# Cached attention as one unrolled line on turned layouts, and grouped attention's values as three products of 256 columns

## The reference, cut to what matters

```python
def _L0_xattn_ref(x, mask, k_cache, v_cache, wq, wk, wv, wo):
    q, k_new, v_new = (jnp.einsum('bsd,ed->bse', x, w) for w in (wq, wk, wv))
    k = jnp.concatenate([k_cache, k_new], axis=1)
    v = jnp.concatenate([v_cache, v_new], axis=1)
    scores = jnp.einsum('bqd,bkd->bqk', q, k) / math.sqrt(256)
    out = jnp.einsum('bqk,bkd->bqd', jax.nn.softmax(scores, axis=-1), v)
    return jnp.einsum('bqd,ed->bqe', out, wo)
...
x = x + _L0_xattn_ref(_layernorm(x), mask, ctx_2048, ctx_2048, wq, wk, wv, wo)      # cached attention
x = x + _L0_ffn_ref(_layernorm(x), ...)       # 32 experts, top 4
x = x + _L1_xattn_ref(_layernorm(x), ctx_2048, ...)   # 16 heads of 128, 4 groups of keys: grouped attention
x = x + _L1_ffn_ref(_layernorm(x), ...)       # weights of -1, 0, 1; 8-bit activations
return x
```

## Time and profile before

| what | us |
|---|---|
| runs shown: median (lowest) | 1720.77 (1715.43) |
| the profiled execution, its own time | 1719.92 |
| its span, first to last instruction | 1718.2 |
| cached attention, until the experts' first transfer | 219.7 |
| grouped attention, about | 1116 |

### The profile page before, as it was taken

The page is one execution under the profiler, slowest core; times in us unless marked ns, Lnnn a source line. Parts: engine busy times, 40 slices in busy tenths (PEclk is TensorE's granted clock), DMA queues, the critical chain, the costliest instruction groups (busy, mean ns, idle before and its releaser), DMA issues. The chain is left out here.

```text
span 1718.2 us, 26126 instructions
## 1 busy us (share of the span) xinstructions
PE 1471.8 (86%) x9363; PEld 1327.4 (77%) x9366; DVE 1185.7 (69%) x2437; ACT 992.3 (58%) x2070; POOL 549.4 (32%) x458
## 2 busy tenths in 40 slices
PE   5788735888867898999999989999999999999945
PEld 4777734887756887888988889888888988888823
DVE  3444556888856877777777767777767777777657
ACT  2434414778744655576666666665656656666626
POOL 1011123344434532243232234332323423222125
PEclk8888966999987999999999999999999999999978
DMA  4111035899931312020010101100201001000010
GB/s 161 39 39 39 1 124 171 294 295 300 317 115 40 65 32 64 7 53 21 28 40 20 52 20 40 41 20 25 67 7 53 20 28 38 12 18 22 23 52 25
DMA packets 79334, 121.40 MB, mean 71 GB/s; under 512 B 16740, under 2 KB 59912, under 8 KB 78696
## 3 DMA queue, kind: packets, MB, share of 16 engines
q1 hardware_dynamic: 74648, 107.28, 19.6%
q0 software_dynamic: 4560, 12.46, 3.1%
HBM read 107.72 MB, written 11.99 MB: 70 GB/s over the span
## 5 line engine op out<-in xcount | busy, mean ns | idle before, releaser
L1688 ACT ACTIVATE ga_pT<-ga_ps_t 128x512 fp32r<-128x512 f32 (+1 forms) x512 | 243.8, 516 | 242.8 <-PE ga_ps_t L1928 242.1
L1823 DVE TENSOR_TENSOR ga_pT<-ga_ps_t,ga_pT 128x512 fp32r<-128x512 f32 (+1 forms) x512 | 279.9, 582 | 89.8 <-ACT ga_pT L1688 87.5
L1696 ACT ACTIVATE ga_probs<-ga_ps_s,ga_neg_max 128x1200 f32<-128x1200 f32 (+1 forms) x256 | 235.7, 927 | 107.3 <-DVE ga_neg_max L1844 107.0
L1928 PE MATMUL ga_ps_t<-all_eye,ga_probs 128*128 128x128 f32 (+1 forms) x1664 | 227.0, 274 | 3.0 <-DVE ga_pT L1823 3.0
L1928 PEld LDWEIGHTS ga_ps_t<-all_eye,ga_probs 128*128 128x128 f32 (+1 forms) x1664 | 195.2, 141 | 17.7 <-DVE ga_pT L1823 4.7
L1839 DVE TENSOR_REDUCE ga_part_max<-ga_ps_s 128x1 f32<-128x1200 f32 x128 | 178.5, 1394 | 7.8 <-PE ga_ps_s L1879 7.2
L1879 PE MATMUL ga_ps_t<-side_w_kv,side_encT 128*128 128x256 f32 (+1 forms) x1170 | 163.9, 289 | 13.4 <-DVE ga_pT L1823 8.6
L1964 PE MATMUL ga_ps_m<-ga_pT,side_v 128*128 128x512 f32 (+1 forms) x416 | 160.8, 417 | 13.5 <-DVE ga_out_n L1857 13.2
L1879 PEld LDWEIGHTS ga_ps_t<-side_w_kv,side_encT 128*128 128x128 f32 (+1 forms) x1170 | 146.5, 188 | 26.0 <-DVE ga_pT L1823 13.1
L1879 PE MATMUL ga_ps_s<-side_kT,ga_qT 128*128 128x400 f32 (+1 forms) x768 | 159.2, 357 | 5.2 <-ACT ga_probs L1696 5.1
L1964 PE MATMUL ga_ps_m<-ga_pT,ga_v 128*128 128x512 f32 (+1 forms) x416 | 157.9, 411 | 6.0 <-DVE ga_out_n L1857 4.5
(11 more groups left out here) (304 smaller groups left out, 3004.6 us busy)
## 6 DMA issues: line engine op xcount, KB each, us to landing
ex_raw<-in_L_ffn_packed SPq DMA_DIRECT2D x63, 704.0 KB, 6.2
side_w_q_raw<-in_L_xattn_Wq SPq DMA_DIRECT2D x16, 512.0 KB, 4.6
side_w_q_raw<-in_L_xattn_Wo SPq DMA_DIRECT2D x16, 512.0 KB, 4.7
ga_inv_rows<-ga_inv_row SPq DMA_DIRECT2D x64, 128.0 KB, 3.1
mix_y_rows<-ex_y SPq DMA_DIRECT2D x63, 128.0 KB, 4.5
ca_cache<-in_ctx SPq DMA_DIRECT2D x4, 1536.0 KB
side_enc<-in_ctx_turned SPq DMA_DIRECT2D x12, 512.0 KB, 5.1
ca_f_raw<-in_L_ffn_turned SPq DMA_DIRECT2D x3, 1024.0 KB, 11.0
```

Of the source, the lines that this page charges most:

```text
L1688: nc.scalar.activation(dst(HI), src, ACT.Copy, scale=scale).then_inc(read, 1)
L1696: nc.scalar.activation(dst, src, ACT.Exp, bias=neg_max[:, n % 2:n % 2 + 1], accum_out=half_sum[:, n % 4, k:k + 1]).then_inc(exped, 1)
L1823: nc.vector.tensor_tensor(dst(LO), src, f32(dst(HI)), ALU.subtract).then_inc(empty, 1)
L1928: mm = nc.tensor.transpose(out[0:top, i * P:(i + 1) * P], probs[step % PB][:, tile * P:tile * P + top], eye[:, :])
```

## The change

`cached_attention` is written anew in the manner of the grouped attention: 8 steps n (b = n // 2, t = n % 2) and 3 draining ones, a plan that all engines walk, three banks of `ps_t`, three buffers of probabilities. TensorE's program is this plan:

```diff
+    def turned_probs(n):
+        if n % 2 == 0:
+            u, order = n // 2 - 1, [(0, 0), (1, 0), (0, 1), (1, 1)]
+        else:
+            u, order = (n - 3) // 2, [(0, 2), (0, 3), (1, 2), (1, 3)]
+        return [("pT", (t, k), u) for t, k in order] if 0 <= u < B else []
+    def weighed_at(n):
+        u, half = ((n - 3) // 2, 0) if n % 2 else (n // 2 - 2, 1)
+        return [("weigh", (half, piece), u) for piece in range(2)] if 0 <= u < B else []
+    def step_plan(n):
+        b, t = n // QT, n % QT
+        turns, values = turned_probs(n), weighed_at(n)
+        first = [("scores", 0, n)] if n < N else []
+        if t:
+            to = b + 1
+            xT, q, k = ([(kind, 0, to)] if to < B else [] for kind in ("xT", "q", "k"))
+            return first + turns[0:2] + xT + values[0:1] + q + turns[2:3] + k + values[1:2] + turns[3:4]
...
+        return first + turns[0:2] + values[0:1] + turns[2:3] + values[1:2] + turns[3:4] + v + y + f
+    plan = {-1: [("xT", 0, 0), ("q", 0, 0), ("k", 0, 0)]}
```

```diff
+            sp.dma_start(x_sb[:, 0:QT, :], tokens[:, 0:QT, :]).then_inc(x_in, 16)
+            load_weight(Q)
+            load_keys(0)
+            load_weight(K)
+            sp.dma_start(x_sb[:, QT:B * QT, :], tokens[:, QT:B * QT, :]).then_inc(x_rest_in, 16)
+            load_weight(V)
+            load_weight(O)
+            sp.wait_ge(cleared, 1)
+            load_cache(0, 0)
+            load_cache(0, 1)
+            load_ternary(0)
+            load_keys(1)
+            for b in range(1, B):
+                load_cache(b, 0)
+                if b + 1 < B:
+                    load_keys(b + 1)
+                load_cache(b, 1)
+                store_ternary(b - 1)
+                if b < W:
+                    load_ternary(b)
```

```diff
+                        ring(("xT", 0, to))
+                        keys_high(to, 0)
+                        keys_high(to, 1)
+                        ring(("q", 0, to))
+                    for e in turns[2:3]:
+                        ring(e)
...
+                        keys_high(to, 2)
+                        ring(("k", 0, to))
+                    for e in turns[3:4]:
+                        ring(e)
...
+                        keys_high(to, 3)
...
+                        cache_high(b - 1, 1)
...
+                        ternary_sign(b - 1)
```

In the grouped attention:

```diff
-        ps_m = ps("ps_m", [P, 2, S])
+        ps_m = ps("ps_m", [P, S])
...
-                nc.scalar.activation(out_n[:, :], ps_m[:, 1, :], ACT.Copy).then_inc(b_here, 1)
+                nc.scalar.activation(out_n[:, :], ps_m[:, :], ACT.Copy).then_inc(u_here, 1)
...
-            def add_parts(u):
-                dve.wait_ge(b_here, u + 1)
-                nc.vector.tensor_tensor(out_n[:, :], ps_m[:, 0, :], out_n[:, :], ALU.add).then_inc(u_here, 1)
...
-                if n % 2 and 0 <= (n - 5) // 2 < UNITS:
-                    add_parts((n - 5) // 2)
...
-                    nc.tensor.matmul(ps_m[:, :, :], values[0:top, HI, tile, :], pT[0:top, :, tile, :],
-                                     start=tile == 0, stop=False)
-                    mm = nc.tensor.matmul(ps_m[:, 0, :], values[0:top, LO, tile, :], pT[0:top, HI, tile, :],
-                                          start=False, stop=tile == KT - 1)
+                    mm = product(ps_m[:, :], lambda s: values[0:top, s, tile, :], lambda s: pT[0:top, s, tile, :],
+                                 tile == 0, tile == KT - 1)
```

More of the change, by code:

```diff
@@ L82, in cached_attention @@
     ABS_FLOOR = 1e-5
-    assert DC == 2 and QT == 2 and FULL == 12 and NB == 4
+    W, FK = ffn_turned.shape[1], ffn_turned.shape[2]
+    Q, K, V, O = range(4)
+    assert DC == 2 and QT == 2 and FULL == 12 and REST > 0 and FK == 4 * DC * D and W < B
+    blocks = [(k * WIDE, COLS_EVEN if k == NB - 1 else (k + 1) * WIDE) for k in range(NB)]
+    cached = [slice(a, min(z, KV)) for a, z in blocks]
+    assert all((z - a) % 2 == 0 and 0 < z - a <= BANK for a, z in blocks) and EARLY < KV
+    turned_tiles = [range(0, 4), range(4, 8), range(8, 12), range(12, TILES)]
@@ L116, in cached_attention @@
         ps_s = ps("ps_s", [P, NB, BANK])
[L117 to L129, removed]
@@ L138, in cached_attention @@
[L138 to L149, removed]
@@ L173, in cached_attention @@
[L173 to L176, removed]
+        keys_in = [sem(f"keys_in{k}") for k in range(NB)]
+        keys_hi = sem("keys_hi")
+        keys_lo = [sem("keys_lo_pool"), sem("keys_lo_dve")]
+        cache_in = [sem(f"cache_in{h}") for h in range(2)]
+        v_hi = sem("v_hi")
+        v_lo = sem("v_lo")
+        cleared = sem("cleared")
+        normed = sem("normed")
@@ L182, in cached_attention, with row_at, bank_of, filled @@
-        f_signed = sem("f_signed")
+        f_done = sem("f_done")
         f_stored = sem("f_stored")
         block = ctx.enter_context(nc.Block())
-        def rounds(eng, body):
-            for b in range(B):
-                body(b, b == B - 1)
+        STATS, MEANS, VARIANCE, NORMED = QT, 2 * QT, 2 * QT + 1, 3 * QT + 1
+        def row_at(b, stage):
+            return normed, NORMED * b + stage
+        def bank_of(e):
+            return place[e] % TB
+        def filled(e):
+            return full, place[e] + 1
@@ L525 @@
+            pe.wait_ge(cleared, 4)
+            for n in range(-1, N + DRAIN):
+                for e in plan[n]:
+                    if e[0] == "scores":
+                        score(e[2])
+                    elif e[0] == "weigh":
+                        weigh(*e[1], e[2])
+                    elif e[0] in RING:
+                        ring(e)
 class KeySide:
```

738 lines of the change are left out of this document (419 added, 319 removed).

## The result

The launch takes 1700.5 us (median; 1696.4 to 1701.8) against 1720.8 before on the same chip: ratio 0.988, interval [0.9863, 0.9901]. Predicted were 1644 us, and the range ended at 1674. The gain is 20 us instead of 76. With 2% told from no change, as the prediction has it, this is no change, to which it had given 0.03. One execution of the kernel before took 4921.9 us and is left out of its median.

What follows compares the result with a forecast made beforehand. TensorE bounds both attentions: phases following each other in the cached one, its instruction stream with small VectorE gaps in the grouped one. 1719.9 us less 59 (cached) and 17 (grouped) gives 1644 us; range 1620 to 1674.

Steps and rivals of the forecast that it cites:

- TensorE's work in a row, prices and counts: Cached attention: products and transposes priced by distances between starts at full clock; 30 us a row, 120 us for four.
- How well it lets it I take from the grouped attention ... 90%: Cached attention, steps 2 to 7: 80.5 us of TensorE work at the grouped attention's 90% fill takes 89 us.
- Step 2's start at 40: Cached attention, end of the fill: scores of step 2 begin at about 40 us, between 33 and 48.
- The drain, 31 us: Cached attention, steps 8 to 10: 22.8 us of work plus some 8 us standing, 31 us.
- The thirteen others, 7.9 us, stay whole: Grouped attention: thirteen of TensorE's 16 waits for VectorE's addition vanish, a gain of the full 7.9 us.
- the 5.6 at the query transposes: Grouped attention: fourteen query-transpose waits for a low part lose about 0.4 us each, as VectorE is earlier: 5.6 us.
- the three long waits: Grouped attention, where a new row is normalised: 1.2 of each 3.3 us wait stays, a gain of 3.6 us.
- The price of 0.353 us a tile: Grouped attention values: three products of 256 columns take 0.353 us against the old pair's 0.35, so no change.
- E: Rival, grouped attention values: VectorE's lateness returns in full in the next bank wait; 0 instead of 17, 1661 us; chance 0.08.
- C: Rival, grouped attention values: added weight loads not hidden, 83 to 158 us; 1727 to 1802 us; chance 0.04.
- A: Rival, cached attention: ScalarE or VectorE paces, not TensorE; rows of 40 instead of 33 us, 1665 us; chance 0.13.
- B: Rival, cached attention: next row's keys come late behind SP's wait for POOL's split; with fill 1655 us; chance 0.12.

Runs made afterwards that it cites:

- ca_all: Changed kernel plus second ternary buffer, GpSimd's cached split before token scale, ScalarE's last cached copy early, odd-step xT copy before exponentials: launch 1658 to 1660 us.
- cache_early: Changed kernel with ScalarE's last cached-values copy moved earlier in odd steps and ahead of the turned probabilities' copies in the drain: cached stage 199.4 -> 176.4 us.

## Why the prediction was wrong, point by point

The 56 us between 1644 and 1700.5 are, by the stretches of the profiled execution: start 2.3, steps 2 to 7 29.5, drain 7.6, grouped attention 14.2, last stage 2.6.

1. **TensorE's work in a row, prices and counts: right.** 886 instructions (four rows of 220, and six for the ternary sums), the scores 5.3 us a step, 12 products in 1.42 us.
2. **"How well it lets it I take from the grouped attention ... 90%": the step that failed.** The sum of prices, 80.5 us, stood in 118.5, 68%. A share of another stage says what a tuned order reaches, not what this order does. (The share itself is right: 400 and 512 columns at the scores' price are 0.187 and 0.239 us, not 0.182 and 0.232, which makes 1010 us of 1116 and not 1001.) A walk through the queues of the new order was missing, and the new code shows what it would have found: VectorE's norm, GpSimd's split and the ternary passes in one place; SP's ternary load behind a wait for that split; ScalarE's copy at the end of the odd step, needed by TensorE at the start of the next. In ca_all the same 80.5 take 94.8, 85%, so even then the 89 were 6 too few; the drain, 25.8, gives 5 back.
3. **Step 2's start at 40: right** (42.3; 40.2 to 44.3 in the others).
4. **The drain, 31 us: 38.6.** I had allowed 8 us of idle for exponential, copies and result. The two waits for the split cache are 8.5 and their clock 4.0; in ca_all, where both are gone, the drain takes 25.8.
5. **"The thirteen others, 7.9 us, stay whole" and the 5.6 at the query transposes: wrong.** Of the 17.7 us of removed waits some 4 were gained; the others came back at the next waits of the same chain. In one round before, TensorE starts the turned probabilities at 903.66 and goes on with the query transposes at 905.67; after, at 881.53 and 883.54: 2.01 us both times, through ScalarE's copy and VectorE's low part. TensorE came to them earlier, so its wait there is 0.87 instead of 0.58 us. In the three long waits, of which I had counted 3.6 us as gained, VectorE did not even become earlier. After the change, then before it:

```profile
705.25 0.75 POOL L1742 TENSOR_TENSOR ga_out_n<-ga_out_n,ga_inv_rows 128x256 f32<-128x256 f32 x1
705.32 1.15 DVE L1931 TENSOR_SCALAR ga_qn<-all_x,ga_mean_var,ga_rstd 128x256 f32<-128x256 f32 x2 [2.13 <-POOL ga_rstd L1717]
```

```profile
728.14 0.73 DVE L1776 TENSOR_SCALAR ga_qn<-all_x,ga_mean_var,ga_rstd 128x256 f32<-128x256 f32 x2 [2.13 <-POOL ga_rstd L1562]
```

   GpSimd's scaling of the result no longer waits for the addition and starts 0.07 us before the two normalisations, which take 1.15 us instead of 0.73. The reduction begins 1.07 us after the norm's start, where it began 0.98 after it with the addition between. The same stands at all three places (1.15 us each). The price of 0.353 us a tile and the hidden loads were right: 12 products in 1.42 us, each with its load.
6. **The experts at nothing: right** (309.0 against 309.2). The last stage, also at nothing, took 76.1 instead of 73.5; it lies between 73.4 and 76.2 in all runs, with and without either part; in cache_early, with the same last stage, it took 73.4. So I take this for its own spread; no run tested it.
7. **The rivals.** E was nearly right for the grouped attention: 3 or 4 instead of 17. C was wrong. A had the right size for the wrong reason: the two engines' sums were no bound (ScalarE is busy 55 of the 118.5 us, VectorE 62.5; the sign that I had named was 90%), but "stand in one queue behind the exponentials" was a part of it, the smallest. B had the right mechanism, a load late behind SP's wait for GpSimd's split, on the wrong load: the ternary weights, not the keys. I gave each of them a chance as if they excluded one another, and named 1690 only as a sum that would be rare. One stage with three engines' orders new at once had all such delays together here, and the range had to take in their sum.

Of the sum itself: the forecast had 59 us less for the cached stage. In after, TensorE's busy time fell by 19 (163 to 144) and its idle time by 1 (56 to 55). In ca_all, which does get the 59, they fell by 31 (to 132.6, at a granted clock of 0.97 instead of 0.88) and by 28 (to 28.2). So two thirds of the forecast were clock and idle time, which both hang on the order of the queues, and the only term that stood for it was the 90%.

## What to carry to other kernels

Where a rewritten stage's gain is idle time that should vanish, walk one period through every engine's queue, the DMA queue too, and write down beside each instruction what stands ahead of it; a fill share from another stage is no forecast. One late instruction at the end of a step can be paid several times: cache_early moved one copy of 1.26 us in each row and took 22 us away, through TensorE's wait, through SP's queue and through the clock. And a wait that disappears is worth only what the next wait of the same chain doesn't take, so count the chain (scores, largest, exponentials, turns, copies), not the wait.

## What the hardware showed that I had not expected

In these traces VectorE's instructions from SBUF to SBUF and GpSimd's splits exclude each other instruction by instruction. Two tensor_scalar of 256 columns took 4.99 us beside a GpSimd subtraction of 4.58 us, one pass of 2048 took 4.80 instead of 1.29; the two normalisations of the grouped attention took 1.15 instead of 0.73 beside a GpSimd product of 0.75. It goes both ways, and holds for VectorE's subtractions of two SBUF operands as well. From ca_all's timeline:

```profile
104.55 1.12 DVE L467 TENSOR_TENSOR ca_kT<-ca_keys,ca_kT 128x928 fp32r<-128x928 f32 x1
104.65 3.87 POOL L337 TENSOR_TENSOR ca_v<-ca_cache,ca_v 128x1280 fp32r<-128x1280 f32 x1
...
105.60 0.68 DVE L488 TENSOR_TENSOR ca_kT<-ca_ps_t,ca_kT 128x512 fp32r<-128x512 f32 x1
...
107.10 1.87 DVE L467 TENSOR_TENSOR ca_kT<-ca_keys,ca_kT 128x418 fp32r<-128x418 f32 x1
```

GpSimd's split takes 3.87 us instead of 2.9: it begins 0.10 after VectorE's key split and stands until that ends. VectorE's next key split begins beside it and takes 1.87 instead of 0.58: it stands until GpSimd's is done at 108.5. Between them the low part that reads PSUM keeps its 0.68. The Trainium skill has this rule, in its page "SBUF — State Buffer", section "SBUF: two separate sides": one pair of ports is shared by the two engines, whoever starts first has it for the whole instruction, and the other "fully blocks"; VectorE takes it in a two-port mode or with two SBUF inputs. By that rule each of the stops above comes out, if the tensor_scalar passes run in such a mode, which no run here shows by itself; otherwise the trace agrees. I had not held the new GpSimd splits, 11.5 us a row, against it.
